# A two-layer hybrid network on one core: order of adds, norm statistics and logits at the joints of its stages

## What is computed

```python
def _layernorm(x, axis=-1, eps=1e-05):
    m = jnp.mean(x, axis=axis, keepdims=True)
    v = jnp.var(x, axis=axis, keepdims=True)
    return (x - m) / jnp.sqrt(v + eps)

# recurrent block: a scan over segments of 64 tokens, 16 heads of 128
    att_dot = softmax(scores, axis=-1) @ vv
    att_mem = sigma_q @ mem / (sigma_q @ z)
    delta = vv - sigma_k @ mem / (sigma_k @ z)
    mem_new = mem + einsum('bhsk,bhsv->bhkv', sigma_k, delta)
    att = beta * att_mem + (1.0 - beta) * att_dot
    out = att.reshape(Bsz, SEG, H * DV) @ Wo

# feed-forward 0: 8 experts, 2 of them for each token, and a gated shared part
    shared = _silu_and_mul(x @ shared_gate_up_w.T) @ shared_down_w.T
    shared = shared * sigmoid(x @ shared_gate_w.T)
    probs = softmax(x @ gate_w.T, axis=-1)
    routing_weights, selected_experts = top_k(probs, 2)
    for e in range(E):
        w_e = where(selected_experts == e, routing_weights, 0.0).sum(-1)
        combined = combined + w_e[:, None] * (_silu_and_mul(x @ w13[e].T) @ w2[e].T)
    out = shared + combined
# feed-forward 1: the same with an ungated, narrower shared part and the two weights renormalised
```

## Time and profile before

| | us |
|---|---|
| three runs | 1779.51, 1769.38, 1771.57 |
| median | 1771.57 |
| the profiled execution | 1776.44 |
| its span | 1774.3 |

### The profile page before, as it was taken

One profiled execution on the slowest core, in us unless ns is written; L12 is line 12 of the kernel. 1 busy time (PEld: TensorE's weight loads), 2 busy tenths in 40 slices (PEclk: granted clock), 3 DMA queues, 4 the chain that ended last, 5 costly groups with the idle time before them and its releaser, 6 DMA issues. The chain is left out here.

```text
span 1774.3 us, 28070 instructions
## 1 busy us (share of the span) xinstructions
PE 1485.6 (84%) x10122; PEld 1115.1 (63%) x10128; DVE 925.3 (52%) x1996; ACT 769.5 (43%) x1887; POOL 409.1 (23%) x336
## 2 busy tenths in 40 slices
PE   6899999984999589999999789958887794899694
PEld 4777777873777467677676577744444573633473
DVE  5666666664622746565555462273443714366722
ACT  5575656661343243433434334323323242477242
POOL 2507060400253221111101024310000271100173
PEclk9999999997999799999999989977877897899897
DMA  3211020101522200010100051310000533000423
GB/s 104 66 34 58 1 90 2 54 2 57 197 69 93 92 12 30 1 41 0 41 0 1 13 211 62 100 44 1 1 1 1 186 96 115 1 1 1 164 93 116
DMA packets 43781, 99.90 MB, mean 56 GB/s; under 512 B 7312, under 2 KB 22928, under 8 KB 43408
## 3 DMA queue, kind: packets, MB, share of 16 engines
q1 hardware_dynamic: 33680, 69.98, 11.5%
q0 software_dynamic: 9984, 28.32, 4.9%
HBM read 79.93 MB, written 18.35 MB: 55 GB/s over the span
## 5 line engine op out<-in xcount | busy, mean ns | idle before, releaser
L426 PE MATMUL s_bank<-s_expert_w,s_xe 128*128 x368 | 124.9, 462 | 2.1 <-ACT s_xe L542 1.4
L718 DVE TENSOR_TENSOR s_h_e<-s_bank,s_silu_e 128x176 f32<-128x176 f32 x92 | 31.4, 341 | 181.3 <-ACT s_silu_e L548 181.3
L154 POOL MEMSET s_ln_power<- 128x8 f32 x8 | 0.8, 104 | 538.5 <-POOLq L98 538.4
L300 POOL DMA_INDIRECT s_xg<-normed_rows,s_from_row x92 | 91.0, 989 | 123.0 <-DVE s_from_row L672 96.2
L307 POOL DMA_INDIRECT expert_rows<-s_y,s_to_row x92 | 91.1, 990 | 97.5 <-ACT s_y L560 80.4
L1025 ACT ACTIVATE s_scratch<-s_bank,s_neg_max 128x128 f32<-128x128 f32 (+3 forms) x128 | 67.2, 527 | 88.7 <-DVE s_neg_max L1106 88.7
L2337 POOL TENSOR_TENSOR s_w_hi<-s_w_raw,zero 128x1024 fp32r<-128x1024 f32 x25 | 53.5, 2139 | 221.0 <-PE s_memory L80 185.0
L450 PE MATMUL s_bank<-s_expert_w,s_he 88*128 x368 | 95.6, 381 | 4.9 <-ACT s_he L554 4.9
L1106 DVE TENSOR_REDUCE s_neg_max<-s_bank 128x1 f32<-128x128 f32 (+3 forms) x128 | 59.7, 488 | 75.7 <-PE s_bank L934 75.5
L78 PE MATMUL s_bank<-xn_t_hi,s_w_hi 128*128 128x512 f32 x208 | 91.7, 441 | 5.4 <-DVE s_w_lo L1079 4.8
L951 PE MATMUL s_bank<-s_probs_t,s_v 128*128 128x512 f32 (+3 forms) x256 | 76.6, 442 | 19.8 <-ACT s_probs_t L1033 19.8
(11 more groups left out here) (377 smaller groups left out, 4302.7 us busy)
## 6 DMA issues: line engine op xcount, KB each, us to landing
s_expert_w<-in_experts SPq DMA_DIRECT2D x32, 608.0 KB, 12.9
s_w_raw<-in_wa_o SPq DMA_DIRECT2D x16, 512.0 KB, 3.7
s_yg<-expert_rows SPq DMA_DIRECT2D x32, 256.0 KB, 4.6
s_raw<-in_shared SPq DMA_DIRECT2D x16, 384.0 KB, 5.5
normed_rows<-s_ln_xn POOLq DMA_DIRECT2D x8, 512.0 KB, 9.4
s_w_raw<-in_wa_k SPq DMA_DIRECT2D x4, 512.0 KB, 4.0
s_w_raw<-in_wa_v SPq DMA_DIRECT2D x4, 512.0 KB, 3.9
s_w_raw<-in_wa_q SPq DMA_DIRECT2D x4, 512.0 KB, 5.4
```

What stands on the lines that cost most here:

```text
L300: pool.indirect_dma_start(out=xg[:, i % XG_RING, :], out_offset=None, in_=x_rows[:, :], in_offset=bass.IndirectOffsetOnAxis(ap=from_row[:, ...
L426: last = pe.matmul(u_bank[i % 2][:, 0:2 * INTER], xe[:, i % 2, x], expert_of(P, i, w), start=c == 0, stop=c == DC - 1, skip_group_check=True)
```

## The change

1. `Moments`: in stages two to seven of eight, VectorE takes the statistics of the next norm at the end, where rows are final, and GpSimd the root of the first half. The next stage starts by normalising. The first two stages still measure for themselves. The buffers move to `res`.
2. Feed-forward head: all normalising comes before the gate's low part; the weights' high and low parts come behind the norm; logits are made per token tile, xn stationary and 16 gate columns moving, straight into `token_bank`; the two copies and the 16 narrow passes go.
3. ffn0: expert rows are added between the activations of the last two shared chunks, the shared part last, bank by bank.
4. ffn1: clearing, both down chunks and `add_shared` move from before the experts to behind them; then expert rows and statistics.
5. The last stage writes x out in four transfers as pairs of tiles become final; `store_stage` goes.
6. Recurrent stage: `mix` writes `att` (in the place of v) by runs of columns, with a stride of 1 KB between elements that follow each other, once all local attention is done; `o_hi` and `o_lo` hold all heads, written by one contiguous operation for four heads; the projection goes by half of the token runs instead of by batch and alternates with the next group's jobs; `first_deltas` moves behind the first of the jobs; x is reloaded by one transfer (permuted by the host) instead of 32; the store is 16 transfers a group instead of 8, the last group's half of them on ScalarE's queue; the final reload is 4 transfers instead of 1.

The diff, cut:

```diff
+    def stats(self, dve, t):
+        dve.bn_stats(self.res.stats[:, t, :], self.res.x[:, t, :]).then_inc(self.stats_done, 1)
+
+    def moments(self, dve, half):
+        for t in range(half * TB, (half + 1) * TB):
+            self.n_stats += 1
+            dve.wait_ge(self.stats_done, self.n_stats)
+            dve.bn_aggr(self.res.moments[:, t, :], self.res.stats[:, t, :]).then_inc(self.moments_done, 1)
+
+    def root(self, pool, half, ready=False):
+        at = slice(half * TB, (half + 1) * TB)
+        if not ready:
+            self.n_moments += TB
+            pool.wait_ge(self.moments_done, self.n_moments)
+        pool.tensor_scalar(self.res.var[:, at], self.res.moments[:, at, 1], LN_EPS, None, ALU.add).then_inc(self.var_done, 1)
+        self.n_var += 1
+        pool.wait_ge(self.var_done, self.n_var)
+        pool.tensor_tensor(self.res.rstd[:, at], self.res.var[:, at], self.res.power[:, at],
+                           ALU.pow).then_inc(self.rstd_done, 1)
...
+            if not self.measured:
+                dve.wait_ge(self.of.rstd_done, h + 1)
+            elif h == 1:
+                dve.wait_ge(self.of.rstd_done, 1)
...
-                at = slice(half * HALF, (half + 1) * HALF)
-                for c in range(DC):
-                    last = product(pe, logit_bank[half][:], (gate_hi[:, c, :], gate_lo[:, c, :]),
-                                   (res.xh[:, c, at], res.xl[:, c, at]), c == 0, c == DC - 1)
-                last.then_inc(logits_ready, 1)
-            pe.wait_ge(logits_copied, NHALF)
-            for t in range(NT):
-                last = pe.matmul(token_bank[:, t * 16:(t + 1) * 16], logits_t[:, t * P:(t + 1) * P], res.ident[:, 0:16],
-                                 start=True, stop=True, skip_group_check=True)
-            last.then_inc(logits_back, 1)
+                for t in range(half * TB, (half + 1) * TB):
+                    at = slice(t * P, (t + 1) * P)
+                    for c in range(DC):
+                        last = product(pe, token_bank[:, t * 16:(t + 1) * 16], (res.xh[:, c, at], res.xl[:, c, at]),
+                                       (gate_hi[:, c, 0:16], gate_lo[:, c, 0:16]), c == 0, c == DC - 1)
+            last.then_inc(logits_ready, 1)
...
-            clear_acc()
-            down(0, False)
-            for n in range(2, n_first):
-                up(n, 0)
-                up(n, 1)
-                down(n - 1, False)
-            down(n_first - 1, True)
+            if behind:
+                clear_acc()
+                down(0, False)
+                for n in range(2, n_first):
+                    up(n, 0)
+                    up(n, 1)
+                    down(n - 1, False)
+                down(n_first - 1, True)
...
+            pe.wait_ge(he_done, TILES)
+            pe.wait_ge(y_done, TILES)
+            clear_acc()
+            if behind:
                 for n in range(n_first + 1, n_shared):
                     up(n, 0)
                     up(n, 1)
                     down(n - 1, False)
-                down(n_shared - 1, True)
+            else:
+                for n in range(n_shared - 1):
+                    down(n, False)
+            down(n_shared - 1, True)
...
+            def add_tiles(n):
+
+                dve.wait_ge(y_back[n], 16 * TOP_K)
+                dve.wait_ge(acc_read, n + 1)
+                for k in range(TOP_K):
+                    for t in (2 * n, 2 * n + 1):
+                        if k:
+                            dve.wait_ge(y_added, 2 * TOP_K * n + 2 * (k - 1) + t % 2 + 1)
+                        dve.scalar_tensor_tensor(res.x[:, t, :], yg[:, k, t, :], token_w[:, t, k:k + 1], res.x[:, t, :],
+                                                 ALU.mult, ALU.add).then_inc(y_added, 1)
+
+            def measure(n):
+
+                if out is None:
+                    final(dve, n)
+                    for t in (2 * n, 2 * n + 1):
+                        following.stats(dve, t)
+                    if n % 2 == 1:
+                        following.moments(dve, n // 2)
...
+                one, other = range(n_first, n_shared)
+                for half in range(NHALF):
+                    h_of(one, half)
+                for half in range(NHALF):
+                    h_low(one, half)
+                add_tiles(0)
+                h_of(other, 0)
+                add_tiles(1)
+                h_of(other, 1)
+                for half in range(NHALF):
+                    h_low(other, half)
+                add_tiles(2)
+                add_tiles(3)
                 for b in range(4):
-                    add_shared(b, n_shared)
-                dve.wait_ge(acc_read, 8)
-            for t in range(NT):
-                dve.wait_ge(y_back[t // 2], 16 * TOP_K)
-                for k in range(TOP_K):
-                    then(dve.scalar_tensor_tensor(res.x[:, t, :], yg[:, k, t, :], token_w[:, t, k:k + 1], res.x[:, t, :],
-                                                  ALU.mult, ALU.add))
+                    add_shared(b, 2)
+                    if b:
+                        measure(b - 1)
+                measure(3)
...
+            if out is not None:
+                to = out.rearrange("b (t p) d -> p (b t) d", p=P)
+                for n in range(NT // 2):
+                    final(sp, n)
+                    sp.dma_start(to[:, 2 * n:2 * n + 2, :], res.x[:, 2 * n:2 * n + 2, :]).then_inc(stored, 16)
+                sp.wait_ge(stored, 16 * (NT // 2))
...
-                project_out(G, 0)
-                project_out(G, 1)
-                for i in range(2, o_parts):
-                    if more:
-                        job(G + 1, i - 2, False)
+                for i in range(o_parts):
                     project_out(G, i)
+                    if more and i < OVERLAPPED:
+                        job(G + 1, i, False)
...
+            def first_deltas(G):
+
+                dve.wait_ge(v_done, SEGS * G + 1)
+                for u in range(2):
+                    at = slice(2 * u * DH, 2 * (u + 1) * DH)
+                    dve.tensor_copy(delta[:, 2 * u:2 * u + 2, 0:DH], v[:, 0, at].rearrange("p (h n) -> p h n", n=DH)
+                                    ).then_inc(delta_done, 1)
...
-                h = x // 2
+                h, half = divmod(x, 2)
                 dve.wait_ge(read_turned, CHAINS * G + x + 1)
-                dve.wait_ge(dot_done, signals(GROUP * G + h + 1))
-                dve.scalar_tensor_tensor(dot[:, x, :], work[2 + x % 2][:], neg_gate[:, G * GROUP + h:G * GROUP + h + 1], dot[:, x, :],
+                dve.wait_ge(dot_done, signals(GROUP * (G + 1)))
+                dve.scalar_tensor_tensor(att_of(h, half), by_run(work[2 + x % 2][:]), neg_gate[:, G * GROUP + h:G * GROUP + h + 1], by_run(dot[:, x, :]),
                                          ALU.mult, ALU.add).then_inc(att_done, 1)
 
             def low_part(G, i):
-                if i >= 2:
-                    dve.wait_ge(out_done, outs(o_parts * G + i - 1))
-                for b in range(B):
-                    dve.wait_ge(o_hi_done, B * (o_parts * G + i) + b + 1)
-                    dve.tensor_tensor(chain_runs(o_lo[:, i % 2], b), dot_runs(i, b), f32(chain_runs(o_hi[:, i % 2], b)),
-                                      ALU.subtract).then_inc(o_lo_done, 1)
+                dve.wait_ge(o_hi_done, o_parts * G + i + 1)
+                dve.tensor_tensor(part_of(o_lo, i), part_of(att, i), f32(part_of(o_hi, i)),
+                                  ALU.subtract).then_inc(o_lo_done, 1)
```

More of the change, by code:

```diff
@@ L1639, in add_to_stream, with measure @@
                                   ALU.add).then_inc(out_added, 1)
-            norm.statistics(dve)
+            def measure(half, rows_final):
+                dve.wait_ge(out_added, rows_final)
+                for t in range(half * TB, (half + 1) * TB):
+                    following.stats(dve, t)
+                following.moments(dve, half)
             norm.normalise(dve)
```

266 lines of the change are left out of this document (147 added, 119 removed).

## The result

| | before | changed |
|---|---|---|
| median of 12 runs, us | 1779.78 | 1768.47 |
| lowest and highest | 1769.38 to 1783.84 | 1760.70 to 1778.29 |
| ratio, 95% interval | | 0.9949 (0.9926 to 0.9971) |
| span of the profiled execution | 1774.3 | 1763.6 |

Measured again beside the experiments, against 25 runs of the kernel before, the ratio was 0.9994 (0.9971 to 1.0018; median 1774.28). The two intervals touch at 0.9971: the change is worth about 0.3%, some 5 us, where 16.3 were forecast. The time of 1756 was also set against a median of three runs, 1771.57; with twelve it is 1779.78.

The account below looks back on a forecast made before the run. No engine is saturated; TensorE, busy 84%, leads within stages and idles at the joints, so those were priced. Terms summed to -16.3 us: 1760.1 from the profiled run, 1755.3 from the median, stated as 1756, range 1741 to 1774.

Parts of the forecast that it names:

- Heads of the attention stages: Starts of wide, causal and rms stages, rid of 3.2 us of statistics: +0.9, -2.4 and -1.2, together -2.7 us.
- Tails of the attention stages: Ends of wide, causal and rms stages: 1.75 us of statistics exposed in each, plus 0.5 disturbance in all, +5.75 us.
- Feed-forward heads: Four feed-forward starts: less VectorE work ahead against logits per token costing +2.65 us each, together -2.1 us.
- 48 passes at 8.5 us: Feed-forward logits: narrow passes taken half at each clock, 8.5 us against 5.85 for the old form, +2.65 a head.
- ffn0 tails: End of both ffn0 uses: expert-row adds move between activations, statistics take their place; -4.8 us each, -9.6 in all.
- What is late next there is VectorE itself: End of ffn0: VectorE, behind the last product, would finish last, so the -4.8 us a use counts.
- ffn1: Downs moved behind the experts: starts -1.4 us each, -2.8; tails +2.6 in the first use, -1.1 in the last.
- Output: End of the last stage: x stored in pairs when final, only 256 KB behind the last add; -2.0 us.
- recurrent stage: First deltas -3.0, strided mixing +0.4 x 3 and last group -1.0, store -1.5; sum -4.3 us, from -10 to +1.
- B: Rival: head gains swallowed as loads end last at every head, ffn1 starts give nothing; 1765 us; B or D 0.22.
- C: Rival: clock stays low through the 48 passes and up fills, +10 us in each of four heads; 1796 us; chance 0.10.
- D: Rival: downs behind the ffn1 experts run at the lower clock, +4.5 us twice; 1765, joined with B; B or D 0.22.

Follow-up runs that it names:

- tenth experiment: Changed kernel with the rms stage's first-half statistics moved to just before the last add; rms stage 166.8 us against 169.9, ratio 0.9983 to the kernel before.
- second: Changed kernel with the old logits put back (12 products of 512 columns, two copies, 16 narrow passes); ratio 0.9919 to the kernel before.
- eleventh: Changed kernel, statistics still at the tails, with an early GpSimd drain and the old logits; ratio 0.9886 to the kernel before.
- seventh: Changed kernel with every stage's statistics at its head and the old logits; ratio 0.9792 to the kernel before, median 1742.8 us.
- fourth: Changed kernel with every stage taking its own statistics and both roots at its head; ratio 0.9799 to the kernel before.
- eighth experiment: Changed kernel with statistics at the heads, old logits and ffn1's clearing, downs and shared adds before the experts; ratio 0.9807 to the kernel before.

## Why the prediction was wrong

**Heads of the attention stages** (-2.7 forecast). "The wide stage gives nothing and may lose 1.8 to the clock": right at its upper end, +1.5 on the first scores. The step that failed is the rms stage, taken as the middle of 0 and -2.4. It is the same case as the wide one and should have been read as such: first product at the same time, and then the clock, 2 us by the first sum of squares. A load that ends last gives nothing back, and behind the longer idle time the products ran at the lower clock. At the first add of the output product the stage is 2.7 us late. Where no load ends last the step held: in the causal stage the first score products come at 12.9 us instead of 16.3, and at 12.5 to 13.5 in all kernels with a short head (-2.4 forecast).

**Tails of the attention stages** (+5.75). 1.75 us exposed in each: right. The 0.2 to 0.3 us for the first half's statistics "in idle time of VectorE" held in the wide stage (0.3 us between its last two adds) and is the step that failed in the rms stage: 2.9 us in the changed kernel, 1.4 in four of nine profiles (tenth experiment). So the rms stage's +7.4 is 2.7 from the head, 2.9 from here and 1.75 exposed.

**Feed-forward heads** (-2.1). 48 passes at 8.5 us is the mis-sized term for ffn1: 10.4 in both, 7.4 and 8.2 in ffn0. Of the 32 such heads in the eight profiles that have this form with no dense matmul among the passes, 18 took 10.4 us: 13 of the 21 with a short head, 5 of the 11 with a long one. The other error was to price the head's 3.5 us at full worth. Rows known, the mean of the three stages with a moved norm: old logits and short head 29.7 us (second; 29.8 in the eleventh), old and long 30.8 (seventh), narrow passes and short head 31.0 (changed, repeated; 29.7 to 32.0 in the seven profiles of that kind), narrow and long 32.5 (fourth). Three microseconds less of VectorE are worth 1.1 us with the old logits, as the copies then wait for a load; with the narrow passes the spread between profiles is as large as what is left.

**ffn0 tails** (-9.6). VectorE's part was right: from the last product to its last instruction it is 6.0 us in both uses instead of 11.6, -5.6 where -4.8 was forecast. "What is late next there is VectorE itself" is the step that failed: GpSimd's drain was, 2.9 us a stage. It shows in the sign that the prediction gave: the idleness before the wide stage's transposes is 11.8 us and not 9.7, that is 17.7, less 5.6 at the tail and 3.2 at the head, plus 2.9. The row was in the trace of before, in a view that the prediction did not read; it had priced the root as hidden beside the next half, and not what stands behind it on its engine. In the first ffn1 it cost 2.3.

**ffn1** (-2.8 at the front, +1.5 at the back). The front was right in kind: 2.0 us at the last y, by the eighth experiment. In the changed kernel the late list of rows hid it. The back's cover was 1 to 2 us too thin, though the clock there was high (1.00, and not the lower one that the text had feared): the first expert rows are added 8.1 and 7.5 us behind the last y, past the 7 us that the prediction had named as a sign of being wrong.

**Output** (-2.0) and **recurrent stage** (-4.3). From the last add to the end of the span it is 3.5 us instead of 6.2, -2.7, a little better; the last stage as a whole was 1.3 us less good, as its head and its experts gave 2 us less than forecast. In the recurrent one mixing and deltas were right or better (-2.1 a group against -1.1), and the store, -1.5, was +2.0.

**Rivals.** What happened is mostly B, the swallowed gains, with the passes of C at the lower clock (and the up products behind them for some 5 us) in both uses of ffn1. C's price didn't follow, as the first expert tile waits for the list of rows and not for those products. D did not happen. B lost its weight by an argument that did not hold: that VectorE "released the transposes in all heads shown". It did, but the transposes are not the end of a head.

**Left open.** When the clock rises in a head is not explained. It stays low from the stage's start for up to 22 us, in kernels with the same code there by different lengths, and no experiment here decides it: with 48 passes both kinds of head gave 7.3 us in some stages and 10.4 in others. Without them it rose 8 to 10 us into the stage in all four heads of the seventh experiment.

## What to carry to other kernels

Work that is moved from the head of a stage to the tail of the one before is paid in full at the tail and returned at the head only if nothing else, a load above all, ends there at the same time; idle time made in front of TensorE is not neutral: in the wide and the rms stage what followed it ran at the lower clock. An engine's program order can bring in such a load: two copies queued behind a weight split cost 4.4 us of TensorE's time. Before putting an instruction last on an engine, look at the drain behind it: on GpSimd after its own transfers it was 5.1 us, and one drain issued early made the last one 1.15. The version with ffn0's adds, the ffn1 order, the store and the recurrent stage of the change, but statistics at the heads and the old logits, is the one to keep: 0.979. (With ffn1's old order it is 0.981, which the runs can't tell from it.)

## What the runs showed of the hardware

- GpSimd's closing drain: 5.1 to 5.2 us in a stage in which it gathers and scatters, also 14 and 20 us behind the last of them, and 1.15 us when it has drained behind them; 1.14 to 1.15 us behind a root in the changed kernel's attention stages, which have no gathers or scatters.
- Narrow passes of 16 columns with a load of 128 each take 0.12 us at the high clock and 0.21 at the lower, and in 18 of 32 heads the clock stayed at 0.50 through 10.4 us of them with TensorE busy all the time, in both uses of ffn1 also with one dense matmul of zeros in seven.
- A 512-column operation of VectorE takes 0.70 us contiguous and 1.04 with an output stride of 1 KB.
- In ten profiles with the same code there the causal stage took between 204.8 and 214.8 us; a single profile says nothing on a few microseconds there.
